# The experts' last block of 64 units with its low part under its high part, and the router's weights with both parts in one product

## The reference, cut to what matters

```python
gate_base = xf @ Wg.T                  # 704 hidden units
up_base = xf @ Wu.T
base_out = silu(gate_base) * up_base @ Wd.T
router_logits = xf @ Wr.T              # 8 experts
expert_w = (the two largest of softmax(router_logits) kept, the others zero)
for e in range(8):                     # rank 16 each
    h = silu(gate_base + xf @ Ag_e.T @ Bg_e.T * 2) * (up_base + xf @ Au_e.T @ Bu_e.T * 2)
    acc += h @ Ad_e.T @ Bd_e.T * 2 * expert_w[:, e]
return base_out + acc
```

## Time and profile before

| | |
|---|---|
| median of 3 runs | 773.83 us (771.58 to 773.88) |
| the profiled execution | 768.75 us, of which 766.9 us from the first to the last instruction |
| TensorE busy | 705.4 us, 92% of the span, 4014 matmuls |
| VectorE busy | 517.6 us, 67% |
| ScalarE busy | 372.3 us, 49% |
| GpSimd busy | 146.3 us, 19% |
| granted TensorE clock | 0.991 of full speed, mean |

### The profile page before, as it was taken

The page is one execution under the profiler, slowest core; times in us unless marked ns, Lnnn a source line. Parts: engine busy times, 40 slices in busy tenths (PEclk is TensorE's granted clock), DMA queues, the critical chain, the costliest instruction groups (busy, mean ns, idle before and its releaser), DMA issues. The chain is left out here.

```text
span 766.9 us, 10570 instructions
## 1 busy us (share of the span) xinstructions
PE 705.4 (92%) x4014; PEld 589.3 (77%) x4014; DVE 517.6 (67%) x929; ACT 372.3 (49%) x776; POOL 146.3 (19%) x129
## 2 busy tenths in 40 slices
PE   1789999879999999999999999998779999999967
PEld 1568888768878788887888778986658888877857
DVE  3545566985975567555575565757558978889786
ACT  3578676644744325344253433456445354553431
POOL 7424254510000010000100001000132202213340
PEclk9999999999999999999999999999999999999979
DMA  5048443000000000000000000320000000000000
GB/s 178 0 137 302 125 129 93 26 0 1 1 1 1 1 0 1 1 1 1 0 1 1 1 1 0 132 89 1 1 0 1 1 28 1 27 2 1 29 0 28
DMA packets 21282, 25.78 MB, mean 34 GB/s; under 512 B 976, under 2 KB 19408, under 8 KB 20464
## 3 DMA queue, kind: packets, MB, share of 16 engines
q1 hardware_dynamic: 20576, 23.79, 9.4%
q10 hardware_dynamic: 656, 1.31, 0.5%
HBM read 22.94 MB, written 2.16 MB: 33 GB/s over the span
## 5 line engine op out<-in xcount | busy, mean ns | idle before, releaser
L1133 DVE TENSOR_TENSOR h_raw<-h_s,bank 128x512 f32<-128x512 f32 x104 | 71.4, 686 | 125.9 <-ACT h_s L1123 110.0
L1123 ACT ACTIVATE h_s<-bank 128x512 f32<-128x512 f32 x104 | 62.0, 596 | 170.3 <-PE bank L91 170.2
L1138 DVE TENSOR_TENSOR h_ring_lo<-h_raw,h_ring_hi 128x512 fp32r<-128x512 f32 x104 | 77.0, 740 | 0.1
L1127 ACT ACTIVATE h_ring_hi<-h_raw 128x512 fp32r<-128x512 f32 x104 | 64.7, 622 | 1.0 <-DVE h_raw L1133 1.0
L89 PE MATMUL bank<-l_xT_hi,l_wgu 128*128 128x512 f32 x128 | 53.3, 416 | 10.4 <-DVE l_h L2302 10.3
L90 PE MATMUL bank<-fused_lo,h_ring_hi 128*128 128x256 f32 (+1 forms) x224 | 62.6, 280 | 0.0
L89 PE MATMUL bank<-f_yT_hi,mlp_hi 128*128 128x512 f32 x128 | 51.8, 405 | 2.1 <-DVEq L1589 1.2
L2063 ACT ACTIVATE l_s<-bank 128x512 f32<-128x512 f32 x32 | 19.1, 597 | 68.9 <-PE bank L91 68.8
L90 PE MATMUL bank<-l_xT_lo,l_wgu 128*128 128x512 f32 x128 | 52.2, 408 | 0.0
L91 PE MATMUL bank<-l_xT_hi,l_lo 128*128 128x512 f32 x128 | 52.0, 406 | 0.0
L91 PE MATMUL bank<-f_yT_hi,fused_lo 128*128 128x512 f32 x128 | 50.1, 391 | 0.0
(11 more groups left out here) (334 smaller groups left out, 2031.2 us busy)
## 6 DMA issues: line engine op xcount, KB each, us to landing
m_W<-m_scratch SPq DMA_DIRECT2D x16, 512.0 KB, 6.4
fused_raw<-in_fused SPq DMA_DIRECT2D x1, 3584.0 KB, 16.4
res<-in_x SPq DMA_DIRECT2D x4, 512.0 KB, 6.2
fused_raw<-in_fused SPq DMA_DIRECT2D x2, 1024.0 KB, 8.4
l_raw<-in_layer SPq DMA_DIRECT2D x1, 2048.0 KB, 8.5
out_x<-res SPq DMA_DIRECT2D x16, 128.0 KB, 1.8
l_raw<-in_layer SPq DMA_DIRECT2D x1, 1280.0 KB, 12.4
fused_raw<-in_fused SPq DMA_DIRECT2D x1, 1152.0 KB, 5.1
```

Of the source, the lines that this page charges most:

```text
L1123: self.nc.scalar.activation(self.s[u % 2][r, :], gate[r, :], ACT.Silu).then_inc(self.silu.sem, 1)
L1127: self.nc.scalar.activation(self.unit(i, u)[0], self.product(i, u), ACT.Copy).then_inc(self.hi.sem, 1)
L1133: self.nc.vector.tensor_tensor(out=self.product(i, u), in0=self.s[u % 2][r, :], in1=up[r, :], op=ALU.mult).then_inc(self.hidden.sem, 1)
L1138: self.nc.vector.tensor_tensor(out=lo, in0=self.product(i, u), in1=f32(hi), op=ALU.subtract).then_inc(self.lo.sem, 1)
```

## The change

**The last block's h.** For a packed unit, VectorE writes the low part not into the slot's second tile but into partitions 64 to 127 of the first, under the high part. The host lays the last 64 rows of `Wd` and `Ad` down twice, one copy under the other, where zeros stood. One matmul over 128 partitions then gives high by high plus low by high (of h and the weight's high part). A second one over 64 partitions adds the high part of h by the weight's low part. Two matmuls stand in place of three, in `down` for u = 21, 23 and 25. For t = 0 the two alternate, chunk by chunk.

**The router.** Its 8 high columns and 8 low columns stand side by side, and one product with 16 columns loaded makes both; it is done for the high and the low part of x, 4 matmuls in place of 6. The result is 16 x 512. `turn_router` no longer transposes but multiplies by `halves`, a constant of 16 x 8 that adds the two halves: four matmuls with fp32 operands, 16 x 128 loaded, 16 x 8 streamed. `halves` is made by one VectorE instruction ahead of batch 0. The router's weights become a piece of their own (16 columns), so there is one more split on ScalarE and on VectorE in batch 0 and "ranks" has 64 columns fewer.

```diff
     def unit(self, i, u):
-        return cut(self.ring[(i * self.units + u) % self.slots], slice(0, self.rows(u)), slice(None))
+        n, at = self.rows(u), (i * self.units + u) % self.slots
+        return (self.ring[at][0][0:n, :], self.ring[at][1][:, :]) if n == P else (self.ring[at][0][0:n, :], self.ring[at][0][n:2 * n, :])
...
-        piece("ranks", g.ffn_w, 0, at[2])
+        self.known["router"] = len(pieces) + 1
+        logits = g.ffn_w[0][:, 0:FFN_ROUTER].rearrange("p (k t e) -> p k t e", k=KD, e=E)
+        raw = g.fused_raw[:, MLP_ALL:MLP_ALL + FFN_ROUTER].rearrange("p (k t e) -> p k t e", k=KD, e=E)
+        pieces.append(Piece(logits[:, :, 0], logits[:, :, 1], raw[:, :, 0], group(MLP_ALL + FFN_ROUTER)))
+        piece("ranks", g.ffn_w, at[1], FFN_RANKS)
...
                     for c in range(C):
-                        last = product(nc, acc[c // 2][:, c % 2 * D:(c % 2 + 1) * D], cut(h, a, chunk(c)), w, u == 0 and c % 2 == 0, False)
+                        o = acc[c // 2][:, c % 2 * D:(c % 2 + 1) * D]
+                        if packed(u):
+                            nc.tensor.matmul(o, hid.whole(i, u)[:, chunk(c)], w[0], start=False, stop=False, skip_group_check=True)
+                            last = nc.tensor.matmul(o, h[0][:, chunk(c)], w[1][0:FT], start=False, stop=False, skip_group_check=True)
+                        else:
+                            last = product(nc, o, cut(h, a, chunk(c)), w, u == 0 and c % 2 == 0, False)
...
-                    last = product(nc, low_bank[t - 1][:, :], cut(wad, slice(0, width(b)), b), h, b == 0, b == FB - 1)
+                    if packed(u):
+                        nc.tensor.matmul(low_bank[t - 1][:, :], wad[0][:, b], hid.whole(i, u)[:, :], start=False, stop=False, skip_group_check=True)
+                        last = nc.tensor.matmul(low_bank[t - 1][:, :], wad[1][0:FT, b], h[0], start=False, stop=True, skip_group_check=True)
+                    else:
+                        last = product(nc, low_bank[t - 1][:, :], cut(wad, a, b), h, b == 0, False)
...
                 for k in range(KD):
-                    last = product(nc, turn_bank[0][0:EW, :], cut(wr, a, k), cut(xT, a, k), k == 0, k == KD - 1)
+                    for part in range(2):
+                        last = nc.tensor.matmul(turn_bank[0][0:2 * E, :], wr[:, k], xT[part][:, k], start=k == 0 and part == 0, stop=k == KD - 1 and part == 1,
+                                                skip_group_check=True)
...
                 for c in range(C):
-                    last = nc.tensor.transpose(turn_bank[0][:, c * EW:(c + 1) * EW], lg[:, chunk(c)], ident[0:EW, 0:EW])
+                    last = nc.tensor.matmul(turn_bank[0][:, c * E:(c + 1) * E], lg[:, chunk(c)], halves[:, :], start=True, stop=True)
...
+            nc.vector.tensor_tensor(out=halves[:, :], in0=ident[0:2 * E, 0:E], in1=ident[0:2 * E, E:2 * E], op=ALU.add).then_inc(xs_ready.sem, 1)
             norm_x(0, 0)
             norm_x(0, 1)
```

More of the change, by code:

```diff
@@ L1111, in __init__, with whole @@
             self.raw.append(Map(nc, m.at - 4 * S)(f"{name}_raw{n}", [P, S]))
+    def whole(self, i, u):
+        return self.ring[(i * self.units + u) % self.slots][0]
     def unit(self, i, u):
-        return cut(self.ring[(i * self.units + u) % self.slots], slice(0, self.rows(u)), slice(None))
+        n, at = self.rows(u), (i * self.units + u) % self.slots
+        return (self.ring[at][0][0:n, :], self.ring[at][1][:, :]) if n == P else (self.ring[at][0][0:n, :], self.ring[at][0][n:2 * n, :])
     def product(self, i, u):
@@ L1247, in fused_phase @@
     at = opening.at
-    wr = shaped(part(g.ffn_w, at[0], FFN_ROUTER), "p (k e) -> p k e", k=KD)
+    wr = g.ffn_w[0][:, 0:FFN_ROUTER].rearrange("p (k e) -> p k e", k=KD)[:, :, 0:2 * E]
     wa = shaped(part(g.ffn_w, at[1], FFN_RANKS), "p (k n r) -> p k n r", k=KD, n=2)
@@ L1262, in fused_phase @@
     splitting, known = opening.splitting, opening.known
-    SPLIT = {0: ("mlp3",), 1: ("ranks", "mlp4"), 2: ("mlp5",), 3: ("mlp_down4",), 4: ("mlp6",), 5: ("mlp7",), 6: ("base0",), 7: ("expand",), 8: ("down",), 9: ("squeeze",), 11: ("base2",), 12: ("back",)}
+    SPLIT = {0: ("mlp3",), 1: ("router", "ranks", "mlp4"), 2: ("mlp5",), 3: ("mlp_down4",), 4: ("mlp6",), 5: ("mlp7",), 6: ("base0",), 7: ("expand",), 8: ("down",), 9: ("squeeze",), 11: ("base2",), 12: ("back",)}
     SPLIT_NEXT = {15: (0, 2), 17: (2, 3), 19: (3, 4), 20: (4, 6), 21: (6, 7), 23: (7, 8), 24: (8, 9)}
@@ L1275, in fused_phase @@
     xs, ys = over("f_xs", [P, C, D]), over("f_ys", [P, C, D])
-    lg = Map(nc, spread_at + 4 * C * D)("f_lg", [EW, S])
+    lg = Map(nc, spread_at + 4 * C * D)("f_lg", [2 * E, S])
     op0 = [m.pair("f_op0", [P, S])]
@@ L1283, in fused_phase @@
     small = [m(f"f_small{n}", [P, C * E]) for n in range(7)]
+    halves = m("f_halves", [2 * E, E])
     tiny = [m(f"f_tiny{n}", [P, C]) for n in range(7)]
@@ L1298, in fused_phase @@
     yT_t, yT_hi, yT_lo = opening.yT_t, opening.yT_hi, opening.yT_lo
-    xs_ready, xT_t, xT_hi, xT_lo = (sg("f_" + n, 2) for n in ("xs", "xTt", "xThi", "xTlo"))
+    xs_ready = sg("f_xs", 2, 1)
+    xT_t, xT_hi, xT_lo = (sg("f_" + n, 2) for n in ("xTt", "xThi", "xTlo"))
     lg_ready, lg_copied, lgT, centred, exped = (sg("f_" + n, 1) for n in ("lg", "lgc", "lgT", "cent", "exp"))
@@ L1397, in down @@
                         known_weights(i, "down")
-                        w = cut(wd, slice(0, width(b)), b)
+                        w = cut(wd, a, b)
                     for c in range(C):
-                        last = product(nc, acc[c // 2][:, c % 2 * D:(c % 2 + 1) * D], cut(h, a, chunk(c)), w, u == 0 and c % 2 == 0, False)
+                        o = acc[c // 2][:, c % 2 * D:(c % 2 + 1) * D]
[4 more added lines that the diff above has]
+                            last = product(nc, o, cut(h, a, chunk(c)), w, u == 0 and c % 2 == 0, False)
                 else:
@@ L1509, in copy_router @@
                 act.wait_ge(lg_ready.sem, lg_ready.at(i, 1))
-                nc.scalar.activation(lg[:, :], turn_bank[0][0:EW, :], ACT.Copy).then_inc(lg_copied.sem, 1)
+                nc.scalar.activation(lg[:, :], turn_bank[0][0:2 * E, :], ACT.Copy).then_inc(lg_copied.sem, 1)
             def high_ranks(i, n):
@@ L1590, in _ @@
             per_token = lambda t: t[:, :].rearrange("p (c e) -> p c e", e=E)
-            lgv = turn_bank[0][:, 0:C * EW].rearrange("p (c e) -> p c e", e=EW)[:, :, 0:E]
+            lgv = turn_bank[0][:, 0:C * E].rearrange("p (c e) -> p c e", e=E)
             def split(i, u):
@@ L2458 @@
     ranks = lambda a: a.reshape(ER, -1)
+    last_twice = lambda a: _np.concatenate([a, a[:, F - FT:]], axis=1)
     expand = lambda n: f(n).transpose(0, 2, 1).reshape(ER, F)
@@ L2464 @@
                _np.concatenate([expand("Bg"), zeros(ER, FT), expand("Bu")[:, F - FT:], expand("Bu")[:, :F - FT]], axis=1),
-               turned(padded(ranks(f("Ad")), 1, FP), P),
-               turned(padded(f("Wd"), 1, FP), P),
+               turned(last_twice(ranks(f("Ad"))), P),
+               turned(last_twice(f("Wd")), P),
                f("Bd").transpose(0, 2, 1).reshape(ER, D))
```

## The result

The changed kernel takes 777.41 us (median of 6 runs, 776.42 to 779.63), the kernel before 773.29 us beside it (771.58 to 773.88). The ratio is 1.0061, 95% interval 1.0031 to 1.0091: slower by 0.3 to 0.9%, some 4 us. The forecast was 775.4 us, a step of +1.53 us, with "no change" as the likeliest case (0.62, against 0.26 for slower). The time lies in the forecast's range, but a slowdown clear of the scatter was not what it held for likely.

The account below looks back on a forecast made before the run. The prediction took TensorE's pace to bound the fused phase. Its terms, +2.84 - 1.38 - 1.83 + 1.80 + 0.10 = +1.53 us, added to the median 773.83 us gave 775.4 us, range 771.0 to 777.6 us.

Parts of the forecast that it names:

- no change: Whole kernel: time within 0.3% (2.3 us) of the kernel before; chance 0.62.
- (a): Down of u = 21: four matmuls fewer but eight row changes instead of two, +0.71 us a batch, +2.84 us in all.
- (b): Down of u = 23 and 25: one 512-column matmul fewer, -0.23 us, six times on the path, -1.38 us in all.
- (c): Router's product: two matmuls fewer, four times, at 0.228 us each, -1.83 us in all.
- (d): Router's turn: eight fp32 instructions in 0.81 us replace transposes in 0.36 us, +0.45 us each time, +1.80 us in all.
- (e): VectorE and ScalarE: packed low part and router's own piece cost nothing, `halves` ahead of batch 0 costs +0.1 us.
- rival 1: Row alternation at u = 21 is free, starts 0.12 us apart; whole kernel 770.7 us; chance 0.11.
- rival 2: Row alternation at u = 21 is dearer than runs, starts 0.38 us apart; whole kernel 777.4 us; chance 0.17.
- rival 4: The forecast itself: row changes cost about as in runs, (b) partly lost where `turn_x` waits for VectorE; 775.4 us; chance 0.60.
- The upper bound in the text, 0.136: Router's turn: each of eight instructions costs at most 0.136 us, a load of f_lg; 1.09 instead of 0.81 us, sum +2.7 us.

Follow-up runs that it names:

- grouped order: Changed kernel, but u = 21 does its four 128-row matmuls first, then its four 64-row ones; fused phase 379.69 us, ratio 0.9988 to the kernel before.
- all rows: Changed kernel, but the second matmul of a packed unit also goes over 128 partitions; fused phase 378.52 us, ratio 0.9959 to the kernel before.

## Why the prediction was wrong

| step | forecast, us in all | read from the trace | in all |
|---|---|---|---|
| (a) u = 21 | +2.84 | +0.74 a batch | +2.96 |
| (b) u = 23 | -0.69 | +0.06, three times | +0.18 |
| (b) u = 25 | -0.69 | 4.41 us to `turn_x` in both | 0 |
| (c) router's product | -1.83 | -0.45 a batch | -1.80 |
| (d) turn | +1.80 | +0.63 a batch | +2.52 |
| (e) `halves` | +0.10 | one instruction of 0.15 us | +0.1 |
| sum | +1.53 | | +3.96 (the phase: +3.72) |

The 0.24 us between the two last numbers lie in steps of about 0.04 us in other places of the phase; no run explains them.

**(a) and (c) held**, and with them the price of 0.195 us for a change of rows, which the grouped order gave back six at a time. The Trainium skill (TensorEngine Tiling (Array Packing), Key Properties) has the drain at a change of mode; the traces agree for rows, and show none for columns, where 128\*64 and 128\*128 follow one another by 0.23 us after the change too. That free alternation (rival 1) is excluded by steps of 0.31 us, and dearer alternation (rival 2, 0.38 us) as well, although its time, 777.4 us, is the one that was measured: that agreement is chance.

**(b) failed in the sentence "On the path this is so six times."** The step took TensorE's pace as the limit of both places, and missed by 1.56 us. At u = 25 the path to `turn_x` runs over VectorE: the kernel before already waited there, 0.5 us in three, which the view of the earlier trace rows lists further down and the text passed over. The forecast named this loss in rival 4's line but gave it no number in the sum. At u = 23 the row change ahead of the first matmul was the cover of VectorE's low part, with about 0.02 us to spare. The question "what is late next" wasn't asked there. The last sign in the prediction's list of what would be wrong, a new wait of TensorE for a packed low part, is what came about, but the list of waits doesn't show it; only the starts do.

**(e) failed in "the same instruction with another output address: nothing".** It costs no duration (0.69 us), but it starts 0.11 us later, and since it is what u = 23 waits for, 0.11 to 0.12 of the 0.29 us lost there a batch come from it. The Trainium skill (VectorE: DVE Perf Modes, Two Vector instructions with no wait between them) says that an instruction whose output starts in another group of 32 partitions than the last output did is held until the earlier ones have finished. The traces agree, 0.72 us in place of 0.61. The forecast didn't weigh it. The other part of the wait, 0.17 to 0.18 us a batch, stays with the low part in its old place.

**(d) was mis-sized by 0.18 us a batch, in two halves.** "The change of rows in and out stays as it was" is wrong as an account: the 0.36 us that was taken off holds the change back to 128 rows, the 0.81 us of the earlier trace rows doesn't, as 32-row work follows there. That is 0.10 us. The other 0.08 is that 0.81 / 8 = 0.101 isn't the pace of line 436: its instructions start 0.11 us apart too, but for the second, which starts 0.03 us behind the first. The first one's load starts at 48.07, under a matmul of line 433 that also has 32 rows; behind a change of rows the first step takes 0.14 us. The upper bound in the text, 0.136, held. From two narrow windows of the kernel before, behind the first at 48.18:

```profile
48.21 0.47 PE L436 MATMUL bank<-m_row,head_spread 32*128 32x4 f32 x3
48.32 0.47 PE L436 MATMUL bank<-m_row,head_spread 32*128 32x4 f32 x3
```


**The whole time.** +3.72 us on the 773.3 us of before is 777.0, and 777.41 was measured. Had (b) and (d) been sized so, the forecast would have been 775.4 + 1.56 + 0.72 = 777.7 us.

That the cover at u = 23 is thin and that VectorE sets `turn_x` is shown, each by the edit that removes it. The price of the turn is shown by the run with the turn twice and the one with transposes.

## What to carry to other kernels

A matmul saved counts only up to the next place where its engine waits for another one: read the waits behind each saving, the short ones too, and the starts where the list of waits is silent, because a stall under the overlap of two matmuls isn't listed. Mixing row counts cost 0.2 us a change here; giving the second product all 128 rows turned a loss of 0.6% into a gain of 0.4%, and grouping the counts turned it into no measurable change. When two durations are subtracted, both must begin and end at the same kind of neighbour, and a run's length divided by its count is its pace only if all its steps are alike.

## What the hardware showed that was not expected

- VectorE overlapped an instruction with the one ahead of it by 0.08 us when both wrote from partition 0 (0.61 us from start to start, 0.69 long), and not at all when the second wrote from partition 64 (0.72), nor when it wrote from partition 0 behind one that had written from 64 (0.72).
- An fp32 product of 16 x 128 loaded and 16 x 8 streamed is two instructions a call, 0.111 us each; a transpose of 16 x 128 took 0.34 / 4 = 0.085 us with the change of rows shared among four.
- Five of the fourteen profiled executions fell to 1.2 GHz in or behind the wait of 1.7 to 1.85 us in the last batch and lost 0.5 to 1.3 us; in two more the clock fell there without loss, and the others passed the place at 2.4 GHz. With all rows the stretch shows a granted clock of 0.56 and six transposes of 1.48 us, 0.82 elsewhere:

```profile
539.00:542.00 3.00, 2.12 (x7) 1.72 (x8) 1.51 (x3) 0.63 (x1) 0.00 (x0) 0.56 0.00 0
```

```profile
541.33 1.48 PE L1855 MATMUL bank<-ident,l_xs 128*128 128x128 f32 x6
```
